# A transformer block's query and key projections: activations or weights standing, and the way to the attention stacks

## The chip, the cores and the metric

The kernel runs on one core of a Trainium2 chip. The metric is the device time of the whole program in microseconds (us). The core has five engines with a queue each: TensorE (PE) multiplies matrices and writes to PSUM, VectorE (DVE), ScalarE (ACT) and GpSimd (POOL) compute on elements, SyncE (SP) issues the transfers (DMA) between DRAM and SBUF, all from one queue here. A queue is served in order, and the engines wait for each other by semaphores.

## The reference

`x` has 8 batches of 1024 tokens, 256 wide. All is float32.

```
x = x + 0.5 * ffn(layernorm(x))
x = x + attention(layernorm(x))
x = x + 0.5 * ffn(layernorm(x))

attention(x):
    kv_c = rmsnorm(x @ W_kv) * g_kv          # 64 wide
    q_c  = x @ W_q                           # 128 wide
    k_content, v = kv_c @ W_kdec, kv_c @ W_vdec     # 16 heads of 16
    q_content    = q_c @ W_qdec                     # 16 heads of 16
    k_rope, q_rope = rope(x @ W_krope), rope(q_c @ W_qrope)   # 16 heads of 32
    q, k = concat(content, rope)             # 48 per head
    softmax(causal(q @ k.T / sqrt(48))) @ v, all heads @ W_o
rope(x) = x * cos + concat(-x2, x1) * sin    # x1, x2: the halves of the 32
ffn(x) = x @ W.T + b + a mixture of 8 rank-16 experts, the best 2 by a gate
```

## The kernel before, in words

The attention is cut into 32 quads `g`: 4 heads of one batch, 1024 tokens. Each quad's queries and keys lie as stacks in SBUF, the 48 dimensions of a head on partitions and tokens along the row, in two tensors `st[g % 2]` that take turns. To keep float32 precision with the fast one-pass matrix form (fp32r), every value is stored as a high part and a low part: a query stack holds both, 48 rows each, `k1_st` the same, and `k2_st` holds the key's parts exchanged, so that two products (L689 and L691) give a score. One further row carries the shift, minus the largest score of each query, and is multiplied by ones.

A quad passes through these steps, named by their letters in the tables that set the order:

- projection (P, "proj", L740 to L746), one per 128 tokens: the latents of the 128 tokens stand as weights, and `wq_s` (192 columns), `wkr_s` (128, in two products) and `wkv_s` (128) stream past. The result, queries, keys and values in one PSUM bank `wp_b`, has tokens on partitions. ACT copies it (L788, L789) to `qk` and `v_s`, and POOL rotates it (L1058 to L1063).
- turn (T, "turn", L758): four transposes per 128 tokens bring dimensions onto partitions, two heads side by side, in the PSUM bank `tp_b`. ACT writes the high parts (H, L801) and DVE the low parts (L, L910), twice each on 48 partitions. Two transfers of 384 KB for each half of the tokens make `k2_st` of `k1_st` (L578, L579).
- maxima (X on PE at L719, M on DVE at L866 and L869): 48 products of queries with keys, and the largest of each row; then the fold (f), a transpose (F, L725), and the shift goes through DRAM to its row (s on SP, L585 and L589).
- scores (S at L689 and L691, E on ACT at L779), 48 pairs, in the two banks of `st_b`, the mask (K on POOL, L1046), values (V, L707), and the reading of the result (o).

Quads overlap: while the scores of one run, the maxima of the next one or two and the projections of a third stand between them. Beside them run the jobs (J): a job is 512 tokens of the first feed-forward net with the latents, or of the output projection with the second net. Its products all use one PSUM bank, `wj_b`. The latents of a job go to DRAM (`nx_scratch`, `kv_scratch`) and come back as `cur` and `kvc` when the batch before has been projected. The first two jobs run in two lanes side by side, as do the last two; the second lane's buffers lie in `probs`.

What sets the order is a table of letters for each engine, `ORDER`, written out for the whole program (`walk` reads it). PE, for example, takes the next score pair for each S. An instruction's waits follow from what it reads and writes.

## Time and profile before

| | |
|---|---|
| median of 3 runs | 2090.83 us (2090.56 to 2091.69) |
| the profiled execution | 2084.36 us, of which its span (first to last instruction) 2082.6 |
| granted TensorE clock, mean | 0.989 of full |
| busy: PE, PE weight loads | 1996.6 us (96%), 1552.6 (75%) |
| busy: DVE, ACT, POOL | 1665.1 (80%), 1258.9 (60%), 973.2 (47%) |
| DMA | 132.32 MB, mean 64 GB/s |

Busy time is the time in which an engine has at least one instruction running. On PE instructions overlap, so a matmul's duration (start to end) is longer than the distance to the next one. The chain of waits, which follows the work that ended last back through the program, gives that distance. In a row of the groups by line the count of a float32 product is twice that in the code: such a product is two instructions, one with fp32r operands or a transpose is one.

### The profile page before, as it was taken

What the parts mean: (1) busy time and instruction counts of PE and PEld (TensorE: products, weight loads), DVE (VectorE), ACT (ScalarE), POOL (GpSimd) and SP (SyncE); (2) the same over time, 40 slices, a digit from 0 to 9 for tenths busy, and PEclk for the clock granted to TensorE, in tenths of its full rate; (3) what the DMA queues carried; (4) which work ended last, traced back from release to release, by engine and by line L of the source; (5) the groups of instructions that cost most, each with busy time, mean ns of one, the idle gap of its engine ahead of it and who ended that gap; (6) DMA issues with size and microseconds to landing.
All of it is one profiled execution on the core that took longest, in us unless ns stands there. A gap on an engine that the chain in (4) does not pass through costs nothing.

```text
span 2082.6 us, 38517 instructions
## 1 busy us (share of the span) xinstructions
PE 1996.6 (96%) x13248; PEld 1552.6 (75%) x13248; DVE 1665.1 (80%) x4924; ACT 1258.9 (60%) x2857; POOL 973.2 (47%) x1574
## 2 busy tenths in 40 slices
PE   4899999999999999999999999999999999999995
PEld 3677777777777777777877787777777777777654
DVE  4698888888888878888788888888788888888842
ACT  4466676665666656666666665666566665566650
POOL 5554554544545545445444445454454554434421
PEclk9999999999999999999999999999999999999996
DMA  2121311222212322123212232213321232221111
GB/s 80 44 62 45 103 35 47 63 89 82 57 32 69 95 67 57 51 56 107 68 42 72 59 94 60 64 47 101 83 58 32 65 93 73 67 68 42 40 28 43
DMA packets 71665, 132.32 MB, mean 64 GB/s; under 512 B 9840, under 2 KB 28528, under 8 KB 71472
## 3 DMA queue, kind: packets, MB, share of 16 engines
q1 hardware_dynamic: 71472, 129.87, 23.2%
q8 instruction: 106, 1.74, 0.4%
q14 instruction: 87, 0.71, 0.1%
HBM read 40.97 MB, written 38.54 MB: 38 GB/s over the span
## 4 chain that ended last, share of the span: by engine, by line
PE 83%; DVE 7%; DMA 3%; ACT 3%; issue 2%; POOL 1%; SPq 0%; POOLq 0%; DVEq 0%; ACTq 0%
PE mx_b L719 13%; PE st_b L689 13%; PE st_b L691 12%; PE o_b L707 11%; PE wj_b L651 5%; PE tp_b L758 5%; PE wp_b L743 5%; PE wp_b L740 4%; PE wj_b L622 3%; PE wj_b L653 3%; PE wj_b L640 3%; PE wp_b L746 2%; DVE st L910 2%; PE wj_b L633 2%; DMA aoc<-ao_scratch 2%
## 5 line engine op out<-in xcount | busy, mean ns | idle before, releaser
L779 ACT ACTIVATE probs<-st_b 128x512 f32<-128x512 f32 (+3 forms) x1536 | 700.5, 490 | 525.4 <-PE st_b L691 497.3
L689 PE MATMUL st_b<-st 113*128 113x512 f32 (+2 forms) x1536 | 558.1, 369 | 7.9 <-ACT probs L779 5.2
L866 DVE CUSTOM_DVE_ANT_0 mx_b<-mx_b,tri 128x256 f32<-128x256 f32 (+3 forms) x1024 | 512.2, 514 | 51.5 <-PE mx_b L719 43.7
L719 PE MATMUL mx_b<-st 112*128 112x256 f32 (+2 forms) x1536 | 532.7, 390 | 4.0 <-DVE mx_s L866 1.8
L691 PE MATMUL st_b<-st,k_st 112*128 112x512 f32 (+2 forms) x1536 | 527.5, 349 | 0.0
L1058 POOL TENSOR_TENSOR rot_c<-qk,cos_s 128x256 f32<-128x256 f32 x256 | 188.9, 738 | 567.8 <-ACT v_s L789 567.7
L869 DVE TENSOR_REDUCE mx_s<-mx_b 128x1 f32<-128x512 f32 (+1 forms) x512 | 334.5, 653 | 88.5 <-PE mx_b L719 82.6
L910 DVE TENSOR_TENSOR st<-tp_b,st 48x512 fp32r<-48x512 f32 x512 | 352.4, 688 | 44.3 <-ACT st L801 30.7
L719 PEld LDWEIGHTS mx_b<-st 112*128 112x128 f32 x1536 | 272.0, 191 | 111.9 <-issue 53.6
L689 PEld LDWEIGHTS st_b<-st 113*128 113x128 f32 x1536 | 291.3, 190 | 62.4 <-ACT probs L779 22.0
L801 ACT ACTIVATE st<-tp_b 48x512 fp32r<-48x512 f32 x512 | 302.6, 591 | 49.0 <-PE tp_b L758 38.4
L1046 POOL TENSOR_SCALAR_AFFINE_SELECT probs<-probs 128x512 f32<-128x512 f32 x256 | 163.9, 640 | 322.1 <-ACT probs L779 321.9
L691 PEld LDWEIGHTS st_b<-st,k_st 112*128 112x128 f32 x1536 | 292.7, 191 | 21.1
L707 PE MATMUL o_b<-probs,v_s 128*17 128x512 f32 (+3 forms) x3072 | 285.0, 489 | 3.4 <-POOL probs L1046 3.0
L1063 POOL TENSOR_TENSOR qk<-rot_c,rot_s 128x256 f32<-128x256 f32 x256 | 189.0, 738 | 20.1
L707 PEld LDWEIGHTS o_b<-probs,v_s 128*17 128x17 f32 x3072 | 70.5, 96 | 141.2 <-issue 111.1
L758 PE MATMUL tp_b<-ident,qk 128*112 128x128 f32 x1024 | 155.2, 273 | 2.3 <-DVE shift L884 1.9
L743 PE MATMUL wp_b<-wkr_s,cur 128*128 128x128 f32 x1024 | 155.9, 275 | 0.0
L788 ACT ACTIVATE qk<-wp_b 128x384 f32<-128x384 f32 x256 | 126.0, 492 | 44.3 <-PE wp_b L746 41.6
L743 PEld LDWEIGHTS wp_b<-wkr_s,cur 128*128 128x128 f32 x1024 | 147.7, 191 | 0.0
L866 DVE DVE_READ_ACCUMULATOR2_ANT mx_s<- 128x1 f32 x1024 | 137.9, 135 | 2.0
L758 PEld LDWEIGHTS tp_b<-ident,qk 128*112 128x112 f32 x1024 | 121.4, 134 | 22.0 <-issue 5.8
(151 smaller groups left out, 2537.9 us busy)
## 6 DMA issues: line engine op xcount, KB each, us to landing
k_st<-st SPq DMA_DIRECT2D x128, 384.0 KB, 6.1
nx_scratch<-stg SPq DMA_DIRECT2D x14, 768.0 KB, 3.5
cur<-nx_scratch SPq DMA_DIRECT2D x14, 768.0 KB, 4.7
ao_scratch<-o_f SPq DMA_DIRECT2D x256, 32.0 KB, 1.7
xa<-in_x SPq DMA_DIRECT2D x15, 512.0 KB, 4.8
x_scratch<-xa SPq DMA_DIRECT2D x15, 512.0 KB, 2.6
xa<-x_scratch SPq DMA_DIRECT2D x15, 512.0 KB, 4.0
aoc<-ao_scratch SPq DMA_DIRECT2D x15, 512.0 KB, 5.8
```

The source lines that it names most:

```text
L689: nc.tensor.matmul(dst, k1_st[u][0:SHIFT + 1, a, P * j:P * j + P], q_st[u][0:SHIFT + 1, a, q0:q0 + w], start=True, stop=False)
L691: nc.tensor.matmul(dst, k2_st[u][0:SHIFT, a, P * j:P * j + P], q_st[u][0:SHIFT, a, q0:q0 + w], start=False, stop=True).then_inc(st_full, 1)
L707: last = nc.tensor.matmul(o_b[32 * a:32 * a + DV + 1, 0, q0 - HALF * h2:q0 - HALF * h2 + n], v_s[q][:, j, a, :], probs[:, a, PLACE[s]:PLAC ...
L719: nc.tensor.matmul(mx_b[:, m % 2, 0:w], q_st[u][0:SHIFT, a, P * i:P * i + P], k1_st[u][0:SHIFT, a, k0:k0 + w], start=True, stop=True).then ...
L743: nc.tensor.matmul(wp[:, HQ:2 * HQ, DC:DQ], cur[:, k, kk * P:(kk + 1) * P], wkr_s[:, kk, q, :].rearrange("p (a c) -> p a c", c=DR), start= ...
L758: last = nc.tensor.transpose(tp_b[0:TURN, 0, P * c:P * c + P], flat[:, P * c:P * c + TURN], ident[:, :])
L779: nc.scalar.activation(probs[:, a, PLACE[s]:PLACE[s] + n], st_b[:, a % 2, HALF - n:HALF], ACT.Exp, scale=SCALE).then_inc(exp_done, 1)
L801: nc.scalar.activation(heads(st[g % 2][rows], e, k), tp_b[rows, 0, :].rearrange("p (s y n) -> p s y n", s=2, n=P), ACT.Copy).then_inc(hi_d ...
L866: nc.vector.tensor_tensor_reduce(src, src, tri[:, HALF - n:HALF], 1.0, NEG, ALU.add, ALU.max, dst).then_inc(mx_done, 1)
L869: nc.vector.tensor_reduce(dst, src, AX_X, ALU.max).then_inc(mx_done, 1)
L910: last = nc.vector.tensor_tensor(heads(st[g % 2][other], e, k), tp_b[rows, 0, :].rearrange("p (s y n) -> p s y n", s=2, n=P), heads(f32(st ...
L1063: nc.gpsimd.tensor_tensor(d[:, :, DC:DQ], rot_cos, rot_sin, ALU.add).then_inc(roped, 1)
```

## The change

- Weights stand. A job's latents stay in SBUF (`stg`, `kvs`), and a unit is 512 tokens, 8 of the 16 heads, and one side, queries or keys: 64 units. Each has three pieces of 128 rows by 512 tokens: the first halves of the 8 heads' rotated dimensions, the second halves, and the content. A query piece is one product with `wq_s` as weights; of a key unit the first two pieces are two products each with `wkr_s`, the third one with `wk_s`. The weights are sorted into this order once, at the start (ACT, "sort").
- Pieces come out with dimensions on partitions, in `tp_b`. So the turns are gone. ACT copies pieces 0 and 1 ("raw"), the rotation is six operations of 128 by 512 on POOL ("rope"; on DVE for two early units), and high and low parts are made on 128 partitions: the content's from PSUM, the rotated in one instruction of 1024 columns each. The cosines and sines are transposed once into `cos_t` and `sin_t`.
- The stacks come from DRAM: a unit's high and its low part are stored (768 KB each) to `q_scratch` or `k_scratch`, and each half of a quad's `st` is loaded by four transfers of 384 KB, its `k2_st` by two. `k2_st` is one tensor now, not two, and the row of ones is written once.
- Values have products of their own ("v", L834), two of 256 columns per 256 tokens.
- Each lane's jobs have two PSUM banks in turn; `wp_b` is gone.
- The tables of all five engines are new, and the jobs of the two kinds alternate.

```diff
-JOBS = [(JOB_A, 0), (JOB_A, 1)]
-for g in range(QUADS + 2):
-    b, q = divmod(g, NQ)
-    if q < 2 and b + 1 < B:
-        JOBS.append((JOB_A, 2 * b + 2 + q))
-    elif q >= 2 and 0 < b < B - 1:
-        JOBS.append((JOB_C, 2 * b + q - 4))
+for b in range(B - 1):
+    for half in range(2):
+        JOBS.append((JOB_A, 2 * b + 2 + half))
+        if b:
+            JOBS.append((JOB_C, 2 * b - 2 + half))
...
+UNIT = [(m, 0, side) for m in range(2) for side in range(2)] + [(m, 1, side) for m in (1, 0) for side in range(2)]
+UNIT += [(m, pair, side) for m in range(2, 2 * B) for pair in range(NP) for side in range(2)]
...
-        "XXSSVXXSSVXXSSPXSXSJXSXSTSXSXJFSSXXJSSXXTSSXXVSSXXPSSXXTSSVSXXSTSXXSPXSXSVXSXSTSXSXPXSXJSXSXJFSXXSJXXSTJ"
+        "XXSSPXXSSJXSSXPXSXSXJSSXJXSXFSXVXXSSJXXSSPXXSSVXXSSPXSXSPXXSSXPXSSXXFJSXSXPXXSSXVXXSSJXXSSJXXSSVXXSSPXXS"
...
+        def rope(engine, n):
+            r, k = rot[SPARE[n]], in_set(n)[0]
+            cols = slice(HALF * (UNIT[n][0] % 2), HALF * (UNIT[n][0] % 2) + HALF)
+            cs, sn = cos_t[:, cols], sin_t[:, cols]
+            engine.tensor_tensor(r[:, 2, :], r[:, 0, :], cs, ALU.mult)
+            engine.tensor_tensor(r[:, 3, :], r[:, 1, :], sn, ALU.mult)
+            engine.tensor_tensor(r[:, 0, :], r[:, 0, :], sn, ALU.mult)
+            engine.tensor_tensor(r[:, 1, :], r[:, 1, :], cs, ALU.mult).then_inc(rot1[SPARE[n]], 1)
+            engine.wait_ge(rot1[SPARE[n]], k + 1)
+            engine.tensor_tensor(r[:, 2, :], r[:, 2, :], r[:, 3, :], ALU.subtract)
+            engine.tensor_tensor(r[:, 1, :], r[:, 1, :], r[:, 0, :], ALU.add).then_inc(roped[SPARE[n]], 1)
...
+                elif name == "qk":
+                    g, half = n, arg[0]
+                    if g > 1:
+                        sp.wait_ge(exp_done, UNITS * (g - 2 + half) + (0 if half else HQ * 2 * HT))
+                    landed(sp, g, half)
+                    b, q = divmod(g, NQ)
+                    cols = slice(HALF * half, HALF * (half + 1))
+                    for side in range(2):
+                        for hl in range(2):
+                            sp.dma_start(f32(st[g % 2])[DQ * hl:DQ * (hl + 1), side, :, cols],
+                                         qk_d[side][b % 2, hl, HQ * DQ * q:HQ * DQ * (q + 1), cols].rearrange(
+                                             "(a r) t -> r a t", a=HQ)).then_inc(qk_in[g % 2][half], 16)
                 elif name == "k2":
                     g, half = n, arg[0]
-                    sp.wait_ge(tp_free, tp_use("turn", g, HT * half + HT - 1) + 1)
-                    k1, k2, cols = f32(st[g % 2])[:, 1], f32(k2_st[g % 2]), slice(HALF * half, HALF * (half + 1))
-                    sp.dma_start(k2[0:DQ, :, cols], k1[ODD:SHIFT, :, cols]).then_inc(k2_in[g % 2][half], 16)
-                    sp.dma_start(k2[ODD:SHIFT, :, cols], k1[0:DQ, :, cols]).then_inc(k2_in[g % 2][half], 16)
+                    if g:
+                        sp.wait_ge(exp_done, UNITS * (g - 1 + half) + (0 if half else HQ * 2 * HT))
+                    landed(sp, g, half)
...
+                    dst = tp_b[:, 0, :].rearrange("p (t c) -> p t c", c=P)
+                    eight = slice(PH * DP * pair, PH * DP * (pair + 1))
+                    if side == 0:
+                        last = nc.tensor.matmul(dst, wq_s[:, k, eight], own.stg[:, :, 2 * P:3 * P], start=True, stop=True)
+                    elif k < 2:
+                        for kk in range(KD):
+                            last = nc.tensor.matmul(dst, wkr_s[:, kk, k, eight], own.stg[:, :, P * kk:P * kk + P],
+                                                    start=(kk == 0), stop=(kk == KD - 1))
+                    else:
+                        last = nc.tensor.matmul(dst, wk_s[:, eight], own.kvs[:, :, :], start=True, stop=True)
...
+                    dve.wait_ge(hir_done, g + 1)
+                    hi, lo = hl_t[SPARE[g]]
+                    nc.vector.tensor_tensor(lo[:, 0:2, :], rot[SPARE[g]][:, 1:3, :], hi[:, 0:2, :].bitcast(F32),
+                                            ALU.subtract).then_inc(lor_done, 1)
```

On PE near the middle of the program the order before has projections (L740 to L746) and turns (L758) between the maxima (`mx_b`) and score pairs (`st_b`):

```order
L758 MATMUL tp_b<-ident,qk 112x128 x4
L740 MATMUL wp_b<-wq_s,cur 128x4x48
L743 MATMUL wp_b<-wkr_s,cur 128x4x32 x2
L746 MATMUL wp_b<-wkv_s,kvc 128x4x2x16
L719 MATMUL mx_b<-st1 128x256
L719 MATMUL mx_b<-st1 128x512
L689 MATMUL st_b<-st0 128x384
L691 MATMUL st_b<-st0,k2_st0 128x384
```

In the changed kernel two pieces of a key unit stand in such places, each in two products of 512 columns:

```order
L755 MATMUL st_b<-st0 128x512
L757 MATMUL st_b<-st0,k2_st 128x512
L824 MATMUL tp_b<-stg,wkr_s 128x512 x2
L787 MATMUL mx_b<-st1 128x512
L787 MATMUL mx_b<-st1 128x384
L755 MATMUL st_b<-st0 128x512
L757 MATMUL st_b<-st0,k2_st 128x512
L755 MATMUL st_b<-st0 128x512
L757 MATMUL st_b<-st0,k2_st 128x512
L787 MATMUL mx_b<-st1 128x512
L824 MATMUL tp_b<-stg,wkr_s 128x512 x2
```

Between two pieces there is at least a score pair or a maximum, and no transpose of projected values is left. On SP, in the middle of the program, the order before has the exchanged copies (`k2_st`), the shift's two steps and the result's stores for one quad and its neighbour:

```order
L578 DMA k2_st0<-st0 48x4x512
L579 DMA k2_st0<-st0 48x4x512
L585 DMA shift_scratch<-shift 16x128
L589 DMA st0<-shift_scratch 1x4x512
L597 DMA ao_scratch<-o_f 16x512 x4
L578 DMA k2_st1<-st1 48x4x512
L579 DMA k2_st1<-st1 48x4x512
L597 DMA ao_scratch<-o_f 16x512 x4
```

In the changed kernel the queue has, around one quad's loads:

```order
L613 DMA q_scratch<-hi_t 384x1x512
L613 DMA q_scratch<-lo_t 384x1x512
L624 DMA st1<-q_scratch 48x4x512 x2
L624 DMA st1<-k_scratch 48x4x512 x2
L635 DMA k2_st<-k_scratch 48x4x512 x2
L613 DMA k_scratch<-hi_t 384x1x512
L613 DMA k_scratch<-lo_t 384x1x512
L643 DMA shift_scratch<-shift 16x128
L624 DMA st1<-q_scratch 48x4x512 x2
L624 DMA st1<-k_scratch 48x4x512 x2
L647 DMA st0<-shift_scratch 1x4x512
L635 DMA k2_st<-k_scratch 48x4x512 x2
```

Stores of units and loads of stacks now stand among the shift's two steps, and the shift's load (L647) waits for its store (L643) in the same queue as they do.

## Rows read from the trace of the kernel before

**Rows 1.** The page's busy time, share of the span, instructions.
```profile
PE 1996.6 (96%) x13248; PEld 1552.6 (75%) x13248; DVE 1665.1 (80%) x4924; ACT 1258.9 (60%) x2857; POOL 973.2 (47%) x1574
```

**Rows 2.** The page's chain that ended last, share of the span by engine, by line.
```profile
PE 83%; DVE 7%; DMA 3%; ACT 3%; issue 2%; POOL 1%; SPq 0%; POOLq 0%; DVEq 0%; ACTq 0%
PE mx_b L719 13%; PE st_b L689 13%; PE st_b L691 12%; PE o_b L707 11%; PE wj_b L651 5%; PE tp_b L758 5%; PE wp_b L743 5%; PE wp_b L740 4%; PE wj_b L622 3%; PE wj_b L653 3%; PE wj_b L640 3%; PE wp_b L746 2%; DVE st L910 2%; PE wj_b L633 2%; DMA aoc<-ao_scratch 2%
```

**Rows 3.** The steady stretch: length, busy per engine, PEclk, DMA share, GB/s.
```profile
290.00:1764.00 1474.00, 1458.66 (x9841) 1144.76 (x9840) 1231.25 (x3641) 925.65 (x2126) 707.19 (x1149) 1.00 0.25 67
```

**Rows 4.** The chain of waits, 1026 to 1049: start, us, what.
```profile
1026.63 0.33 PE wp_b L740 x2
1026.96 0.45 PE wp_b L743 x4
1027.40 0.22 PE wp_b L746 x2
...
1028.89 0.44 PE tp_b L758 x4
...
1041.58 0.23 PE st_b L689
...
1046.17 0.87 PE wj_b L651 x4
```

**Rows 5.** The same chain near 1184.
```profile
1183.98 1.72 PE wj_b L659 x4
```

**Rows 6.** Groups by line and shape, PE: count, busy, mean ns.
```profile
L743 PE MATMUL wp_b<-wkr_s,cur 128*128 128x128 f32 x1024 | 155.9, 275 | 0.0
L758 PE MATMUL tp_b<-ident,qk 128*112 128x128 f32 x1024 | 155.2, 273 | 2.3 <-DVE shift L884 1.9 <-DVE st L910 0.3
...
L740 PE MATMUL wp_b<-wq_s,cur 128*128 128x192 f32 x512 | 128.7, 332 | 4.5 <-ACT v_s L789 4.1
L651 PE MATMUL wj_b<-w_s,xt 128*128 128x256 f32 x480 | 126.8, 387 | 3.0 <-ACT xn L841 1.7 <-DVE xa L1007 1.3
L746 PE MATMUL wp_b<-wkv_s,kvc 128*128 128x128 f32 x512 | 99.5, 276 | 0.0
...
L659 PE MATMUL wj_b<-stg,wkvq_s 128*128 128x512 f32 x56 | 26.3, 592 | 0.0
```

**Rows 7.** Groups by line and shape, ACT and DVE.
```profile
L801 ACT ACTIVATE st<-tp_b 48x512 fp32r<-48x512 f32 x512 | 302.6, 591 | 49.0 <-PE tp_b L758 38.4
...
L910 DVE TENSOR_TENSOR st<-tp_b,st 48x512 fp32r<-48x512 f32 x512 | 352.4, 688 | 44.3 <-ACT st L801 30.7
```

**Rows 8.** Groups by line and shape, POOL.
```profile
L1058 POOL TENSOR_TENSOR rot_c<-qk,cos_s 128x256 f32<-128x256 f32 x256 | 188.9, 738 | 567.8 <-ACT v_s L789 567.7
...
L1086 POOL TENSOR_TENSOR xn<-hl,gate 128x512 f32<-128x512 f32 x30 | 32.8, 1095 | 18.2 <-DVE gate L999 18.1
```

**Rows 9.** DMA queue q1: packets, MB, share of 16 engines' span.
```profile
q1 hardware_dynamic: 71472, 129.87, 23.2%
```

**Rows 10.** Issues by line: count, KB each, median us to landing.
```profile
k_st<-st SPq DMA_DIRECT2D x128, 384.0 KB, 6.1
nx_scratch<-stg SPq DMA_DIRECT2D x14, 768.0 KB, 3.5
cur<-nx_scratch SPq DMA_DIRECT2D x14, 768.0 KB, 4.7
...
shift_scratch<-shift SPq DMA_DIRECT2D x64, 8.0 KB, 1.3
```

**Rows 11.** Stretches inside k_st copies (1062), inside loads from ao_scratch (1004.5).
```profile
1062.00:1066.00 4.00, 4.00 (x30) 2.20 (x29) 3.42 (x13) 1.68 (x4) 3.84 (x8) 1.00 0.80 180
...
1004.50:1007.00 2.50, 2.50 (x23) 1.49 (x15) 0.94 (x3) 0.46 (x2) 2.42 (x5) 1.00 0.95 320
```

**Rows 12.** PE in order of time: the first projection, the first maximum.
```profile
65.02 0.55 PE L740 MATMUL wp_b<-wq_s,cur 128*128 128x192 f32 x2
...
79.23 0.79 PE L719 MATMUL mx_b<-st 112*128 112x256 f32 x2
```

More of the change, by code:

```diff
@@ L31 @@
 WIDE = 256
-ODD = 64
-SHIFT = ODD + DQ
+SHIFT = 2 * DQ
 HLW = ER + E
@@ L40 @@
 RT = 9
-TURN = ODD + DQ
 FOLD = 72
 CONST = 2
+NP = 2
+PH = H // NP
+DP = DC
 TWO = 96
@@ L118, with uses @@
+def uses(*steps):
+    out = []
+    for n, (m, pair, side) in enumerate(UNIT):
+        out += [(name, n, *arg) for name, *arg in steps]
+        if side and not pair and m:
+            out += [("v", k, tt) for k in ((0, 1) if m == 1 else (m,)) for tt in range(2)]
+    return out
 ORDER = {
     "PE": (
-        "JJJjJjjjJJjJjjJJJJjjjJjPJPJPjJTJPTPXXTXXXXPXXJTXXJXXTPXJXXTPXXPXXFXXTXXXPXXSTSXXSSXXSSXPXTXSSXXSSXPXTXSS"
-        "VXXSSTPXXSSJXPXJXTJXXVTXXJXXPFXXPXXTJXXSSXXPSXSXTSXSXSXSXPSXXFSVXXSSXTXSSXXSSXPXSXSTSXSXJSXXSJSXSXJXXSSJ"
@@ L283 @@
         "X": quads(*[("mx", m) for m in range(NM)]),
-        "P": PROJ,
-        "T": quads(*[("turn", k) for k in range(TB)]),
+        "P": TABLES + uses(("piece", 0), ("piece", 1), ("piece", 2)),
         "F": quads(("mx_turn", 0), ("mx_turn", 1)),
@@ L312 @@
         "j": lane_jobs(1, FFN_POOL + [("aggr", 1), ("ss",)], FFN_POOL),
-        "B": [("blank", 1, k) for k in range(BLANKS)],
+        "w": [("widen", 0)],
     },
     "SP": {
+        "u": [("store", n, hl) for n in range(NU) for hl in range(2)],
+        "q": quads(("qk", 0), ("qk", 1)),
         "k": quads(("k2", 0), ("k2", 1)),
@@ L336 @@
 for name, g, *arg in walk("PE"):
-    if name in ("turn", "mx_turn"):
+    if name in ("table", "piece", "v", "mx_turn"):
         TP_USE[name, g, arg[0]] = len(TP_USE)
@@ L482, in f32, with wj_of, last_use, landed @@
             return tensor[tuple(slice(None) for _ in tensor.shape)].bitcast(F32)
-        def heads(tensor, e, k):
-            return tensor.rearrange("p s (y e) t -> p s y e t", e=2)[:, :, :, e, P * k:P * k + P]
         def count(n, k):
             return sum(LANE[i] == LANE[n] and (k == 0 or JOBS[i][0] == JOB_A) for i in range(n))
-        def latents(n):
-            if n > 1:
-                return stg[:, :, :], kvs[:, :, :]
-            return cur[:, HT * n:HT * n + HT, :], kvc[0:KR, HT * n:HT * n + HT, :]
-        def blank(u, k):
-            row, value = (ODD - 32, 0.0) if k < 6 else (P - 32, 1.0)
-            flat = k2_st[u].rearrange("p a t -> p (a t)") if k in (4, 5) else st[u].rearrange("p s a t -> p (s a t)")
-            c = 2 * T * (k - 4 if k >= 4 else k)
-            return row, flat[row:row + 32, c:c + 2 * T], value
+        def wj_of(n, name):
+            return lanes[LANE[n]].banks[bank_use(n, name) % 2]
+        def last_use(m):
+            return max(tp_use("piece", UNIT_OF[m, NP - 1, 1], 2), tp_use("v", m, 1))
+        def rope(engine, n):
[9 more added lines that the diff above has]
+            engine.tensor_tensor(r[:, 1, :], r[:, 1, :], r[:, 0, :], ALU.add).then_inc(roped[SPARE[n]], 1)
+        def landed(sp, g, half):
+            b, q = divmod(g, NQ)
+            units = [UNIT_OF[2 * b + half, q // (NQ // NP), side] for side in range(2)]
+            if g == 1:
+                units += [n for n in range(NU) if SPARE[n]]
+            for part in range(2):
+                for i in range(2):
+                    mine = [in_set(n)[0] for n in units if SPARE[n] == i]
+                    if mine:
+                        sp.wait_ge(hl_out[i][part], 16 * (max(mine) + 1))
         @block.sync
@@ L580, in _ @@
+                    landed(sp, g, half)
+                    b, q = divmod(g, NQ)
+                    cols = slice(HALF * half, HALF * (half + 1))
+                    for hl in range(2):
+                        sp.dma_start(f32(k2_st)[DQ * (1 - hl):DQ * (2 - hl), :, cols],
+                                     qk_d[1][b % 2, hl, HQ * DQ * q:HQ * DQ * (q + 1), cols].rearrange(
+                                         "(a r) t -> r a t", a=HQ)).then_inc(k2_in[half], 16)
                 elif name == "shift":
@@ L1034, in _ @@
                            allow_small_or_imprecise_dtypes=True)
-            for i in range(NQ):
-                last = nc.gpsimd.memset(v_s[i][:, :, :, :], 1.0)
-            last.then_inc(const, 1)
+            nc.gpsimd.memset(v_s[0][:, :, :, :], 1.0).then_inc(const, 1)
             pool.wait_ge(const, CONST)
             for name, g, *arg in walk("POOL"):
-                own = lanes[LANE[g]]
+                own = lanes[LANE[g % NJ]]
                 if name == "mask":
```

615 lines of the change are left out of this document (330 added, 285 removed).

## The prediction

> **What bounds the kernel now.** I read the page's busy times first: PE has work in 96% of the span, DVE in 80%, ACT in 60% [rows 1]. Then the chain that ended last, since a share of busy time says nothing of who waits: it runs on PE for 83% of the span, on DVE for 7%, and the projections and turns have 5 + 5 + 4 + 2 = 16% of it, the low parts (`st`, L910) 2% [rows 2]. Then one long stretch, 290 to 1764 us: PE is busy for 1458.7 of 1474, at full clock, DVE for 84% [rows 3]. So the middle of the program is a queue of matmuls with hardly a gap, and what leaves that queue is what the change is worth. The reader should then see that a matmul's price is not its duration. A turn lasts 273 ns and the groups give the turns 155.2 us busy [rows 6], but on the chain four of them take 0.44 us, 110 ns each [rows 4], for the rest is overlapped by the next one. I price PE by distances on the chain.
>
> **PE, out.** One projection is 0.33 + 0.45 + 0.22 us, one turn 0.44 [rows 4]: 1.44 us, times 256 is 369 us. That is 18% of the span, near the chain's 16%.
>
> **PE, in.** A float32 product of 512 columns is two instructions, and four of these take 1.72 us [rows 5], 0.43 each. 32 query units of three products and 32 key units of five make 256 products, 512 instructions, 220 us. The values are 64 products of 256 columns, 128 instructions at 0.87 / 4 us [rows 4], 28 us. 16 transposes for the tables, 2 us. Together 250 us. The columns that stream past are as many as before (256 x 576 = 256 x 512 + 64 x 256), so nearly all of the difference, 119 us, is the turns. It counts in full only where PE was the chain; by the chain's 16% instead of 18% it is about 105. I take 112, bounds 100 to 119. Two instructions of 512 columns could also be dearer than in rows 5: busy time over count is 26.3 / 56 = 0.47 us [rows 6], which would take 20 us back; I take the chain's price.
>
> **DVE and ACT.** Out go 512 low-part instructions, 352.4 us, and 512 high-part ones, 302.6 [rows 7]. In come, per unit, one PSUM difference of 512 columns (0.69 us by L910) and one of 1024 (at most twice that): 64 x 2.07 = 132 us, so DVE loses some 220 of its 1665 us. ACT gets 128 raw copies, 64 content parts and 32 value copies of about 0.6 us and 64 copies of 1024 columns, at most 1.2: 211 us, against the 302.6 and the copies out of `wp_b`. The reason is the shape: 128 rows where there were 48. These engines hide behind PE for the most part, so this pays only in the 7% of the chain that is DVE's, 146 us, 2% (42 us) of it L910 itself [rows 2]. Bounds 0 and 146; I take 30, nearest to L910's own share, since the rest belongs to the maxima, which stay.
>
> **POOL.** Out go four operations per projection, two of 738 ns and two of about half the size. In come 62 times six of 512 columns: by L1086 1.1 us each, by doubling L1058 1.48 [rows 8], 409 to 550 us in all against some 600. Nothing is gained, as POOL was 47% busy [rows 1]; but one rotation now holds its queue for 7 to 9 us, and masks stand behind it, for which the value products wait. The order places about one rotation per 30 us; I count this in the new waits below.
>
> **The start.** From the first projection to the first maximum passed 14 us [rows 12]. Now the way is: pieces 0.9 us each, two raw copies 0.6, a rotation 7 to 9, a high part 1, a store 3.5, four loads; `cur<-nx_scratch`, 768 KB, landed in 4.7 [rows 10], so 6 or 7 for twice that. That is about 21 us, 7 later, though query pieces can begin before the key latents are done, and PE has more other work to do first. Bounds 0 and 20; I take 8. The table of letters shows the last two lanes' work nearly as before, and the second PSUM bank can save a microsecond or two there; I take nothing.
>
> **The transfers, where I see the risk.** Stacks: 64 halves x 6 loads of 384 KB = 151 MB; stores: 128 x 768 KB = 101 MB. Out go the copies to `k2_st`, 50 MB, and the latents' way through DRAM, 26 MB. From 132 MB it becomes about 308, 9.6 per quad. The queue's 129.87 MB took 23.2% of the span [rows 9], 3.7 us per MB; at that, 308 MB are 1,146 us, 58% of the new span. Before, no matmul of the middle depended on a transfer of this size just in time. Now four loads fill half of `st` after the scores of the quad two earlier have left it and before the first maximum of the new one. I counted PE's work between these two in the new order with the distances of rows 4 (512-column pairs 0.47 us, a job's products 0.2 each): 12 to 20 us in the steady part, with 13 in one quad of four; for `k2_st`, now single, 15 to 27, for the shift 37 to 42 and 17 to 24. How long the four loads take is not in the trace; the nearest rows are transfers of like rows of 2 KB. The copies to `k2_st`, also on 48 partitions, moved 180 GB/s, loads from `ao_scratch` on 128 partitions 320 [rows 11]. 1.57 MB are 8.7 or 4.9 us, with some 1.3 for a small one's way [rows 10]: 6 to 10 us, within 12. With two stores of the same size in front, 11 to 19, which is within the lead at 320 and over it at 180. I take the faster side, since source and destination are different memories here as for `ao_scratch`, and 10 us in all for new waits (these, `tp_b`'s single bank between pieces, the masks); bounds 0 and 170 (below).
>
> The Trainium skill ("DMA: Bandwidth & Descriptors", section "Anatomy of one DMA") fits a transfer by 2.0 us plus its bytes at 436 GB/s. For 768 KB that is 3.8 us, and the store of `nx_scratch` took 3.5 [rows 10]; for the second of the copies to `k2_st` it would be 3.8 as well, counted from the first, where the row has 6.1. By the rule the four loads would take an estimated 5.6 us and never be waited for; by the copies' row they would take 10. It agrees with my forecast, and the copies' row is the rival's.
>
> **Sum.** Against the profiled execution of 2084.4: -112 (PE) - 30 (DVE on the chain) + 8 (start) + 10 (new waits) = 1960. The median of the runs was 6.5 above that execution, so 1967.
>
> **Rivals.**
>
> *The loads come too late.* Slower than before. For: 2.3 times the bytes, one queue, the shift's load waits for its store in SP's queue (1.3 us in rows 10, several times that behind megabytes) and holds up all that follows; at 180 GB/s 308 MB would take 1,710 us. Then half of the 64 halves have stores in front and wait 19 - 13 = 6 us or so at worst, the others less; with queueing I take 5 us for 32 halves: 160 us, on top of which the forecast's 10 goes. 1967 + 150 = 2117. It decides from a rate under about 220 GB/s. Against: leads of 12 us and more everywhere, and the 320 GB/s row. A milder form, a few us in one quad of four and short waits for `tp_b`, gives +20 to +100, 1990 to 2070.
>
> *Busy time is the right price.* By the groups, out go 155.9 + 155.2 + 128.7 + 99.5 = 539 us, in come 512 x 0.47 + 128 x 0.264 = 274 [rows 6]: 265 less, 1820, as a median 1826. Against: 539 us would be 26% of the span where the chain has 16%. A lesser form, in which most of DVE's 146 us on the chain goes with its load, gives 1967 - 100 = 1870 to 1920.
>
> The Trainium skill ("Trainium Kernel Development and Optimization", section "Performance Expectations") says that matmul busy time is a bad metric, because matmuls are pipelined. The trace agrees, 273 ns against 110 for a turn; whoever took busy times all the same would say 1826.
>
> *The change doesn't thin PE's queue.* Not so here: the order shows 5572 rows on PE for 6350, and no transposes but the jobs', the tables' and the shift's.
>
> **Chances.** The forecast, 1925 to 2005: 0.62. Some waits for loads or banks, 2005 to 2087: 0.16. Within 0.2% of before, which is what a measurement of this kernel can tell from no change: 0.02. Late loads, over 2095: 0.12. Under 1925: 0.08. So faster 0.86, same 0.02, slower 0.12. The range, 1915 to 2070, leaves out late loads and the busy-time price; the likeliest case alone is 1925 to 2005.
>
> **What would show it.** In the new trace: four 512-column instructions on the chain in 1.72 us, and no other line's distance changed; PE busy near 96 to 98% with about 110 us less; L910's kind of work at some 130 us and DVE under 76%; no line of waits of PE for a DMA on `st` or `k_st` over some 10 us in total; DMA share near 0.55 to 0.6; the first maximum at about 87 us. Wrong would be: PE idle before L787 or L755 for DMAs for tens of us, landing times of the `st` loads over 12 us, or a PE queue that stands at the pieces for ACT's copies out of `tp_b`.

## The result, and the profile after

| | before | changed |
|---|---|---|
| median (range) | 2090.69 us (2087.92 to 2091.69) | 2005.82 us (2005.07 to 2010.95) |
| ratio, 95% interval | | 0.961, 0.959 to 0.963 |
| profiled execution; its span | 2084.36; 2082.6 | 2005.28; 2002.8 |
| granted clock, mean | 0.989 | 0.980 |

The changed kernel is 85 us faster. The forecast was 1967, so it misses 39 us of what was expected, inside the range of 1915 to 2070. The page of the changed kernel, its busy times and its chain by engine and by line, answers to [rows 1, 2]:

```profile
PE 1901.2 (95%) x10832; PEld 1325.5 (66%) x10832; DVE 1439.5 (72%) x4555; ACT 1024.3 (51%) x2125; POOL 849.4 (42%) x912
...
PE 68%; DMA 10%; DVE 8%; POOL 7%; ACT 2%; issue 2%; SPq 1%; POOLq 0%; DVEq 0%; ACTq 0%
PE st_b L755 12%; PE o_b L775 11%; PE mx_b L787 11%; PE st_b L757 10%; PE tp_b L824 4%; PE wj_b L712 4%; DMA st<-k_scratch 3%; PE tp_b L821 3%; PE wj_b L681 2%; PE wj_b L714 2%; DMA q_scratch<-lo_t 2%; PE wj_b L699 2%; DVE xn L1077 2%; PE wj_b L692 2%; DVE mx_b L977 1%
```

PE lost 95 us of busy time, DVE 226, ACT 235. The chain ran on PE for 83% of the span and now for 68%: DMA and POOL have taken 17% of it where they had 4%. The steady stretch, 290 to 1700, with the columns of [rows 3]:

```profile
290.00:1700.00 1410.00, 1381.70 (x8063) 974.61 (x8056) 1061.65 (x3351) 751.93 (x1578) 636.16 (x673) 1.00 0.65 162
```

PE is busy for 98.0% of it, 99.0% before, and DVE for 75%, 84% before. The chain of waits near 1203 has the price of the new products, as [rows 4, 5]:

```profile
1201.87 0.23 PE st_b L755
1202.10 0.23 PE st_b L757
...
1203.10 0.86 PE tp_b L821 x2
```

The groups by line and shape, to be held against [rows 7, 8]:

```profile
L1030 DVE TENSOR_TENSOR lo_t<-rot,hi_t 128x1024 fp32r<-128x1024 f32 x62 | 78.3, 1264 | 21.7 <-ACT hi_t L907 21.4
...
L1025 DVE TENSOR_TENSOR lo_t<-tp_b,hi_t 128x512 fp32r<-128x512 f32 x62 | 42.4, 684 | 16.2 <-DMA q_scratch<-lo_t 10.7 <-ACT hi_t L901 5.3
...
L907 ACT ACTIVATE hi_t<-rot 128x1024 fp32r<-128x1024 f32 x62 | 65.6, 1058 | 104.3 <-POOL rot L529 104.1
...
L523 POOL TENSOR_TENSOR rot<-rot,cos_t 128x512 f32<-128x512 f32 x62 | 79.1, 1276 | 148.6 <-ACT rot L872 148.5
```

and from the page, over all shapes, the value products:

```profile
L775 PE MATMUL o_b<-probs,v_s 128*17 128x512 f32 (+3 forms) x3072 | 285.7, 490 | 2.0 <-POOL probs L1169 1.9
```

The low parts take some 121 us where they took 352. ACT stands at the high parts for POOL's rotation, 104 us in 52 of them, and DVE at the low parts for ACT. The DMA queue and the issues, as [rows 9, 10]:

```profile
q1 hardware_dynamic: 169648, 305.53, 61.0%
...
st<-q_scratch SPq DMA_DIRECT2D x128, 384.0 KB, 5.9
st<-k_scratch SPq DMA_DIRECT2D x128, 384.0 KB, 8.7
k_st<-k_scratch SPq DMA_DIRECT2D x128, 384.0 KB, 10.4
```

PE's waits for these loads, from the list of waits (us in all, times, longest), are small:

```profile
PEld mx_b L787 <- DMA st<-k_scratch: 4.4, 7, 1.2
...
PE mx_b L787 <- DMA st<-k_scratch: 2.5, 4, 1.0
```

**Where the 85 us are.** The two profiled executions differ by 80 us. I divided each at the first maximum of quad 4 and that of quad 28; the end goes to PE's last instruction. Between the two maxima I added PE's instructions at their usual distance at full clock (0.43 us for 512 columns as one of the two instructions of a float32 product, 0.11 for a transpose, and so on) and call the rest PE's waits; some 15 us of these stand ahead of value products in every kernel.

| us | to quad 4 | 24 quads | PE's work in them | PE's waits in them | the end |
|---|---|---|---|---|---|
| before | 289.8 | 1474.3 | 1401.9 | 72.4 | 313.9 |
| changed | 302.4 | 1400.7 | 1307.1 | 93.7 | 295.2 |

So the work left as priced (95 of an expected 24/32 x 119 = 89 us), but the waits, which I had expected to fall, rose by 21, and the start took 13 us more. (Profiled executions of kernels with the same start differ there by up to 4 us.) Spread evenly over the quads, with the start's 8 us outside them, the forecast's saving of 124 us is an estimated 99 in the 24 quads and 25 outside; measured are 74 (95 less 21) and 6.

**The clock is part of these waits.** The granted clock fell from 2.4 to 1.2 GHz for short stretches, and what PE lost there counts as waiting above. The changed kernel has three of them in the 24 quads, at 903.0, 1107.8 and 1578.8 us; PE, busy for 98% of the steady stretch, had been busy for 5.0 of the 7.0 us ahead of the first and for 5.9 of the 7.8 ahead of each of the others. The first one, as a stretch with the columns of [rows 3], then on the chain:

```profile
903.00:906.40 3.40, 3.40 (x7) 2.04 (x8) 1.97 (x11) 0.60 (x1) 1.25 (x2) 0.50 0.05 16
```

```profile
902.94 0.98 PE mx_b L787 x2
903.91 0.43 PE st_b L755
904.35 0.42 PE st_b L757
904.77 1.71 PE tp_b L821 x2
```

A score product takes 0.43 us there for 0.23, two pieces' instructions 1.71 for 0.86. All such stretches together, from the clock records of each trace (us at the lower level):

| us at 1.2 GHz | to quad 4 | in the 24 quads | the end |
|---|---|---|---|
| before | 10 | 3 | 31 |
| changed | 37 | 10 | 31 |

At most half of a stretch is lost. So the changed kernel lost up to 17 us more to the clock than the kernel before, up to 14 of them before quad 4, where its start is 13 us longer. Where the clock fell after PE had stood, a wait cost twice; how much of the start's 13 us is the one and how much the other, no run separates.

### The profile page after: what moved, and what is told of

The parts are those of the page before. It is cut to its first block, busy times and chain, and to the rows that moved or that the text cites. A ratio compares the mean times of both kernels' runs of the same rounds, so it can differ in the third digit from the quotient of the medians.

```text
span 2002.8 us, 32215 instructions
## 1 busy us (share of the span) xinstructions
PE 1901.2 (95%) x10832; PEld 1325.5 (66%) x10832; DVE 1439.5 (72%) x4555; ACT 1024.3 (51%) x2125; POOL 849.4 (42%) x912
## 4 chain that ended last, share of the span: by engine, by line
PE 68%; DMA 10%; DVE 8%; POOL 7%; ACT 2%; issue 2%; SPq 1%; POOLq 0%; DVEq 0%; ACTq 0%
PE st_b L755 12%; PE o_b L775 11%; PE mx_b L787 11%; PE st_b L757 10%; PE tp_b L824 4%; PE wj_b L712 4%; DMA st<-k_scratch 3%; PE tp_b L821 3%; PE wj_b L681 2%; PE wj_b L714 2%; DMA q_scratch<-lo_t 2%; PE wj_b L699 2%; DVE xn L1077 2%; PE wj_b L692 2%; DVE mx_b L977 1%
## 5 line engine op out<-in xcount | busy, mean ns | idle before, releaser
L755 PE MATMUL st_b<-st 97*128 97x512 f32 (+2 forms) x1536 | 588.2, 387 | 10.6 <-ACT probs L859 6.8
L787 PE MATMUL mx_b<-st 96*128 96x256 f32 (+2 forms) x1536 | 565.5, 411 | 12.4 <-DVE mx_s L980 6.3
L757 PE MATMUL st_b<-st,k_st 96*128 96x512 f32 (+2 forms) x1536 | 533.4, 351 | 0.0
L787 PEld LDWEIGHTS mx_b<-st 96*128 96x128 f32 x1536 | 282.0, 191 | 169.6 <-issue 80.1
L755 PEld LDWEIGHTS st_b<-st 97*128 97x128 f32 x1536 | 293.1, 191 | 134.7 <-issue 61.4
L757 PEld LDWEIGHTS st_b<-st,k_st 96*128 96x128 f32 x1536 | 294.9, 192 | 33.0 <-issue 9.8
L712 PE MATMUL wj_b<-w_s,xt 128*128 128x256 f32 x480 | 123.9, 380 | 1.3 <-ACT xn L951 1.3
L824 PE MATMUL tp_b<-stg,wkr_s 128*128 128x512 f32 x240 | 114.9, 601 | 1.6 <-ACT rot L872 0.9
L1192 POOL TENSOR_TENSOR xa<-xa,hb_s 128x256 f32<-128x256 f32 x120 | 93.1, 802 | 24.8 <-DVE xn L1077 24.8
L1077 DVE TENSOR_SCALAR xn<-xa,mv,rs 128x256 f32<-128x256 f32 x180 | 95.4, 577 | 7.0 <-POOL rs L1185 5.8
## 6 DMA issues: line engine op xcount, KB each, us to landing
k_st<-k_scratch SPq DMA_DIRECT2D x128, 384.0 KB, 10.4
```

What stands on the lines that cost most here:

```text
L712: nc.tensor.matmul(dst, xt[:, tk, P * kk:P * kk + P], w1_s[:, kk, 0:D], start=(kk == 0), stop=False)
L755: nc.tensor.matmul(dst, k1_st[u][0:SHIFT + 1, a, P * j:P * j + P], q_st[u][0:SHIFT + 1, a, q0:q0 + w], start=True, stop=False)
L757: nc.tensor.matmul(dst, k2_st[0:SHIFT, a, P * j:P * j + P], q_st[u][0:SHIFT, a, q0:q0 + w], start=False, stop=True).then_inc(st_full, 1)
L787: nc.tensor.matmul(mx_b[:, m % 2, 0:w], q_st[u][0:SHIFT, a, P * i:P * i + P], k1_st[u][0:SHIFT, a, k0:k0 + w], start=True, stop=True).then ...
L824: last = nc.tensor.matmul(dst, wkr_s[:, kk, k, eight], own.stg[:, :, P * kk:P * kk + P], start=(kk == 0), stop=(kk == KD - 1))
L1077: last = nc.vector.tensor_scalar(own.xn[:, tk, :], own.xa[:, tk, :], own.mv[:, tk, 0:1], own.rs[:, tk:tk + 1], ALU.subtract, ALU.mult)
```

## The experiments

Ratios are to the kernel before, run on the same chip; the changed kernel's is 0.961. More, faster and slower by so many us are against the changed kernel, for few_turns against the kernel before: the difference of the two ratios times 2088 us, good to some 5 us. "Waits" are those of the 24 quads as above, from one profiled execution each, and hold what the clock took: the 24 quads had no stretch at 1.2 GHz in few_turns, add_turns and short_rope, 10 us in light_loads, free_high and shift_first as in the changed kernel, 24 in dve_even, 27 in early_rope, 31 in late_low and one_bank, 48 in late_high and 65 in dve_back. Up to half of each figure is in the waits.

**The turns put back, in the changed kernel.**

```diff
+                    for c in range(5):
+                        nc.tensor.transpose(tp_b[:, 0, P * (c % 4):P * (c % 4) + P], ident[:, :], ident[:, :])
                     dst = tp_b[:, 0, :].rearrange("p (t c) -> p t c", c=P)
```

> The changed kernel with five transposes of 128 columns (of the identity, into tp_b, overwritten by the piece that follows) ahead of each of its 192 pieces: PE gets back about the instructions that the turns were, 960 of 0.11 us by the distances on the chain, 106 us, and no other engine gets any work. Theory A (PE's queue is what the kernel is made of, also after the change, and work in it counts in full): 90 to 110 us more than the changed kernel. Theory B (the removed instructions had partly filled time in which PE would have waited for DVE or ACT, so the waits grew when they went, some 20 to 30 us): the same instructions put back hide those waits again, 60 to 85 us more. Theory C (transfers set the pace of the changed kernel): under 50 us more.

2062.6 us, ratio 0.988 (0.986 to 0.990), 56 us more. That is between theory C and the 60 to 85 of theory B. Half of the 106 us came back as time. In the 24 quads PE's work grew by 78 us and its waits fell by 34, from 94 to 60.

**Turns taken out, in the kernel before.**

```diff
-                    for c in range(HALF // P):
+                    for c in range(HALF // P if g < 2 else 1):
                         last = nc.tensor.transpose(tp_b[0:TURN, 0, P * c:P * c + P], flat[:, P * c:P * c + TURN], ident[:, :])
```

> The kernel before, in which from the third quad on one of the four transposes of a turn is made (the result is not the reference's); 720 transposes of 0.11 us by the distances on the chain are gone, 79 us, and nothing else. Theory A (instructions leaving PE's queue count in full): 72 to 80 us faster than before. Theory B, after add_turns, where 106 us came out as 57: a part of the turns filled time in which PE would wait for DVE and ACT, whose load is larger here than in the changed kernel: 25 to 50 us faster.

2057.1 us, ratio 0.984 (0.982 to 0.986): 33 of 79 us. In the 24 quads the work shrank by 63 us, the waits grew by 38. Both runs say the same, and the lists of waits show where. PE's weight loads for the maxima, waiting for DVE to empty a bank, in the kernel before:

```profile
PEld mx_b L719 <- DVE mx_s L869: 17.8, 36, 0.9
...
PEld mx_b L719 <- DVE mx_s L866: 11.8, 34, 0.9
```

in the kernel before with fewer turns:

```profile
PEld mx_b L719 <- DVE mx_s L869: 28.7, 65, 0.9
PEld mx_b L719 <- DVE mx_s L866: 26.0, 85, 0.9
```

in the changed kernel:

```profile
PEld mx_b L787 <- DVE mx_s L977: 30.9, 98, 2.3
PEld mx_b L787 <- DVE mx_s L980: 26.9, 65, 2.5
```

and in the changed kernel with the turns put back:

```profile
PEld mx_b L787 <- DVE mx_s L979: 17.6, 54, 1.2
PEld mx_b L787 <- DVE mx_s L982: 11.4, 32, 1.5
```

30, 55, 58, 29 us: the sum follows the turns, whichever kernel they stand in. For the score pairs, waiting for ACT, it is 22, 40, 46 and 28. So it is theory B's mechanism in both runs: the turns were filler for PE's waits as much as work.

**DVE's load put back, in lumps and evenly.** Six maxima of 512 columns per unit, two behind the content's low part and four behind the rotated one's:

```diff
+                    if extra[0]:
+                        dve.wait_ge(ex_done, extra[0])
+                    for e in range(4):
+                        nc.vector.tensor_reduce(ex_s[:, e:e + 1], cos_t[:, HALF * (e % 2):HALF * (e % 2) + HALF],
+                                                AX_X, ALU.max).then_inc(ex_done, 1)
+                        extra[0] += 1
...
```

> The changed kernel with six additional maxima of 512 columns per unit on DVE (read from cos_t, result unused), two behind the content's low part and four behind the rotated one's: some 0.6 us each, 3.6 per unit, 220 us more busy on DVE, which is what the change took from it. PE, ACT, POOL and the transfers get nothing. Theory A (of the prediction, the load taken from DVE paid about 30 us): 25 to 50 us more. Theory B (DVE's load was hidden by PE's queue and taking it paid nothing): under 10 us more. Theory C (DVE's load is what the maxima wait for, so that a us of it shows nearly in full): 100 us or more.

2160.9 us, ratio 1.035 (1.033 to 1.038), 155 us more, slower than the kernel before. Waits 216, of which 110 ahead of maxima (20 in the changed kernel). Next, the same work singly (`if m % 4 == 3:` behind a maximum, one `tensor_reduce`):

> As dve_back the changed kernel with some 220 us of additional maxima on DVE (384 of 512 columns, 0.6 us each, from cos_t, unused), but single, one behind every fourth maximum, where dve_back had lumps of 1.2 and 2.4 us behind the low parts and came out 155 us slower. Theory A (DVE's queue is long in all, so what it is given shows wherever it stands): 100 us slower or more. Theory B (a lump longer than two banks of maxima can cover was the cost): 20 to 60 us slower.

2038.4 us, ratio 0.976 (0.974 to 0.978), 31 us more; waits 121, 35 ahead of maxima. DVE was busy for 1656 us in the one and 1620 in the other. So it is theory B of the second run: the lump was the cost, by a factor of five. While DVE is away for 1.2 or 2.4 us, PE fills the two banks of `mx_b` and stands. Up to 27 us of the 122 by which the waits of dve_back exceed the changed kernel's are the clock (65 us at 1.2 GHz for 10), the most of all runs.

**Loads lightened.**

```diff
+                            part = slice(HALF * half, HALF * half + 16) if hl and g > 1 else cols
-                            sp.dma_start(f32(st[g % 2])[DQ * hl:DQ * (hl + 1), side, :, cols],
+                            sp.dma_start(f32(st[g % 2])[DQ * hl:DQ * (hl + 1), side, :, part],
...
```

> The changed kernel in which, from the third quad on, the loads of the low parts (of st and of k2_st) move 16 of 512 columns: of 151 MB of loads about 70 are not moved, and the low parts in the stacks are stale, so the result is not the reference's. The number of transfers and of waits stays. Theory A (after the start the loads are never late): within 6 us of the changed kernel. Theory B (the loads, or the bytes in the way of the shift and of the stores, hold back the scores or take time from the other engines): 20 us or more faster.

1987.8 us, ratio 0.952 (0.951 to 0.954), 18 us faster: between the two theories, nearer to B. Waits 81, so 12 of the 18 us are in the steady part. No engine worked faster (DVE 1436.0 us busy, ACT 1025.0, POOL 849.6), so the bytes cost only by coming late, and not at PE alone: DVE's wait for the store of a low part (`lo_t <- DMA q_scratch<-lo_t`), 10.7 us in the changed kernel, is gone, and that for a job's input (`bst <- DMA xa<-in_x`) is 7.1 for 10.4. And the chain by engine of this kernel reads:

```profile
PE 78%; POOL 8%; DVE 8%; ACT 2%; DMA 2%; issue 2%; SPq 0%; POOLq 0%; DVEq 0%
```

DMA's share went from 10% to 2%, 160 us of chain for 18 us of time: a second chain lay close behind it.

**Rotations shortened.**

```diff
-            engine.tensor_tensor(r[:, 3, :], r[:, 1, :], sn, ALU.mult)
-            engine.tensor_tensor(r[:, 0, :], r[:, 0, :], sn, ALU.mult)
...
-            engine.tensor_tensor(r[:, 2, :], r[:, 2, :], r[:, 3, :], ALU.subtract)
```

> The changed kernel with three of the six operations of each rotation left out (the result is not the reference's): POOL holds its queue for some 3.7 us per unit where it was 7.5, about 230 us of its load go. Theory A (POOL's rotations are off the chain, except at the start, where one stands between the first piece and the first maximum): 4 to 10 us faster, all of it before 300 us. Theory B (masks behind the rotations, and ACT, whose queue stands at the high part while POOL rotates, 104 us in sum, hold back the scores): 20 to 50 us faster, spread over the whole span.

1966.2 us, ratio 0.942 (0.940 to 0.945), 39 us faster. Quad 4 begins 11 us sooner, and waits are 66: 27 us of the gain are in the steady part. Theory B in size, but it doesn't tell the masks from ACT's queue, nor either from the unit's way to DRAM. Three runs were to do that.

**High and low parts that don't wait for the rotation.**

```diff
+                        act.wait_ge(roped[SPARE[g]], in_set(g)[0])
...
-                    act.wait_ge(roped[SPARE[g]], done + 1)
+                    if g < 12:
+                        act.wait_ge(roped[SPARE[g]], done + 1)
...
-                    nc.scalar.activation(hl_t[SPARE[g]][0][:, 0:2, :], rot[SPARE[g]][:, 1:3, :], ACT.Copy).then_inc(hir_done, 1)
+                    src = rot[SPARE[g]][:, 1:3, :] if g < 12 else cos_t[:, :].rearrange("p (a t) -> p a t", t=HALF)
+                    nc.scalar.activation(hl_t[SPARE[g]][0][:, 0:2, :], src, ACT.Copy).then_inc(hir_done, 1)
...
```

> The three left-out operations of short_rope gave 40 us, 27 of them in the steady part. Here POOL keeps all six, but from unit 12 on ACT's high part of the rotated pieces (hi_r) and DVE's low part (lo_r) read cos_t, which nobody writes, instead of the rotation's result, so neither waits for POOL (the result is not the reference's); the next unit's first copy waits for the rotation instead. Theory A (ACT's queue stands at hi_r until POOL has rotated, the exponentials behind it come late, and the scores wait for st_b): 15 to 30 us faster than the changed kernel, and PE's waits ahead of score pairs fall. Theory B (the masks and the router's work behind a rotation in POOL's queue come late): within 6 us of the changed kernel, since POOL's queue is the same.

1998.1 us, ratio 0.956 (0.954 to 0.959), 10 us faster, with an interval of about 4 to 16: neither theory's number. Waits ahead of score pairs fell from 21 to 14 us, as A has it, and those of the steady part as a whole from 94 to 88. ACT's standing is a part, not the whole, of short_rope's 39.

**ACT's high parts up to three exponentials later.** The table of letters for ACT, here one of its rows (H is the high part of the rotated pieces, E an exponential):

```diff
-        "EEJEECEECEECEEEEHEEJCEEEECEEJEECEEJEEJHEEEEJEECEEJEECEECEECEEJEECEEHEEEEEEEECEEEECEEJJEECEEHJEEJEEEECEEJ"
+        "EEJEECEECEECEEEEEEHJCEEEECEEJEECEEJEEJEEEHEJEECEEJEECEECEECEEJEECEEEEEHEEEEECEEEECEEJJEECEEHJEEJEEEECEEJ"
```

> Only ACT's table is changed: 39 of the 64 high parts of rotated pieces stand up to three exponentials later (never past a copy or a job's step, so 25 stay); all is computed. Theory A (ACT stands at them for POOL): these 39 no longer wait, 8 to 20 us faster than the changed kernel. Theory B (masks or the router's work on POOL are what is late): within 5 us. Theory C (the units' way to DRAM has no slack, so that a later high part makes a later store and a later load): 5 us or more slower.

2077.5 us, ratio 0.994 (0.992 to 0.996), 69 us slower: four fifths of the gain of the change are gone, though only 39 letters moved, each by two or three places. Waits 153, 52 ahead of maxima. Its list of waits has DVE's standing at the low parts, 21.4 us in the changed kernel:

```profile
DVE lo_t L1030 <- ACT hi_t L907: 82.4, 39, 5.4
```

So it is theory C in sign, and its mechanism is at least in part a lump again: DVE stands at the low part and the maxima behind it wait. Up to 19 us of it in the 24 quads are the clock (48 us at 1.2 GHz for 10).

**DVE's low parts up to two maxima later.** One row of DVE's table (L a low part, every second one a rotated one; M a maximum, o a step of reading the result); 44 of the 64 moved:

```diff
-        "MMnMLMMooMMoJoMMJJJJMMJJMMJJMMJMMfMMnMMMMLMoMMooLoJMMJMMJJJMMJJMMMMMMMMMLMMMMLMMJMMfJJMMnJMMJoMMoJMMoJMM"
+        "MMnMMMLooMMoJoMMJJJJMMJJMMJJMMJMMfMMnMMMMLMoMMoooLJMMJMMJJJMMJJMMMMMMMMMLMMMMMMLJMMfJJMMnJMMJoMMoJMMoJMM"
```

> The changed kernel with DVE's table changed: 44 of the 64 low parts of rotated pieces (lo_r) stand up to two maxima (or a step of reading the result) later. late_high, where ACT made the high parts up to three exponentials later, came out 72 us slower, and DVE then stood for 82 us at lo_r where it had stood for 21. Theory A (a step that stands in DVE's queue before its high part is there holds back the maxima behind it): the 21 us go, 3 to 12 us faster than the changed kernel. Theory B (what counted in late_high was the unit's way to DRAM getting longer): 3 to 15 us slower, as the stores and the next unit's copies come later still.

2022.2 us, ratio 0.968 (0.966 to 0.970), 14 us slower. Theory A fails, and the size is theory B's: letting DVE do maxima first only moved the cost. Waits ahead of a half's first maximum, which needs the loads, went from 3 to 8 us, and those of the shift's transpose from 7 to 11. The way from unit to stack seems to have no slack either; but up to 10 of the 14 us are the clock (31 us at 1.2 GHz for 10), so this is argued and not shown.

**The start: the first shift ahead of the second quad's loads.** SP's table; s is a step of the shift, q and k are loads:

```diff
-        "JjJJjuuuuquuuukqqsqsuukJuuJ
+        "JjJJjuuuuquuuuksqsqquukJuuJ
...
```

> The changed kernel with SP's table alone changed at one place at the start: the first quad's first shift (its store and its load) stands ahead of the second quad's eight loads, not behind them. Theory A (at the start the shift's two transfers of 8 KB, 9.4 and 7.2 us in the changed kernel, lie behind megabytes, and the first scores wait for them): the first score comes 8 to 12 us sooner, and the whole is 3 to 10 us faster, the less the second quad's loads then come late. Theory B (the start is paced by what comes before, latents, pieces and rotations): within 3 us.

2011.8 us, ratio 0.964 (0.963 to 0.966), 7 us slower, which neither theory has. The changed kernel's chain of waits between the first maxima and the first score has this:

```profile
104.03 0.29 DVE shift L995
104.34 9.38 DMA shift_scratch<-shift
113.74 7.22 DMA st<-shift_scratch
121.00 0.80 PE st_b L755
```

and the chain of this run, where the shift goes first:

```profile
103.77 0.29 DVE shift L995
104.08 0.32 SPq L643
...
105.89 8.95 DMA st<-k_scratch
...
114.89 0.70 PE mx_b L787
```

PE's order has maxima of the second quad ahead of the first scores. Their loads now started late, and the first score began at 129.6 for 121.0. The 16.6 us of two small transfers had been in plain view on the chain, and weren't to be had by moving them alone.

**One bank for the stages again.**

```diff
-            return lanes[LANE[n]].banks[bank_use(n, name) % 2]
+            return lanes[LANE[n]].banks[bank_use(n, name) % 2 if n < 4 or LANE[n] else 0]
...
-                if name == "wo0" and use:
+                if (name == "wo0" or n >= 4 and not LANE[n]) and use:
```

> The changed kernel, in which the first lane's jobs from the fifth on use one PSUM bank again, as before the change, in the same order of work. Theory A (of the prediction, which gave the second bank nothing): within 5 us of the changed kernel. Theory B (the jobs' products stand in the order so that a bank must be free sooner than it can be read): 15 us slower or more, with PE waiting at wj_b.

2029.1 us, ratio 0.974 (0.972 to 0.975), 26 us slower. Theory B: waits 115, the 21 more standing ahead of the jobs' products (10 before `low1`, 5 before `tr1`, where the changed kernel had next to none). Up to 10 of the 21 are the clock (31 us at 1.2 GHz for 10).

**The rotation begun with the first piece.** The one version that was meant to be better:

```diff
+            engine.wait_ge(tp_free, tp_use("piece", n, 0) + 1)
             engine.tensor_tensor(r[:, 2, :], r[:, 0, :], cs, ALU.mult)
+            engine.tensor_tensor(r[:, 0, :], r[:, 0, :], sn, ALU.mult)
+            engine.wait_ge(tp_free, tp_use("piece", n, 1) + 1)
             engine.tensor_tensor(r[:, 3, :], r[:, 1, :], sn, ALU.mult)
-            engine.tensor_tensor(r[:, 0, :], r[:, 0, :], sn, ALU.mult)
...
```

> The changed kernel, all computed, in which the two operations of a rotation that read piece 0 alone come first and wait for piece 0's copy only; the other four wait for piece 1's, as all six did. POOL has the same work. It stood at rotations for piece 1's copy for 148.5 us in 47 of them, 3.1 us each, and two operations are 2.5 us. Theory A (the length of a unit's way from its pieces to the stacks is what the waits grow from: 3.7 us off each rotation gave 40 us, late_high's lengthening cost 72): 2 us off most rotations, 12 to 28 us faster than the changed kernel, masks no later than before. Theory B (short_rope gained by taking load from POOL, so that masks and the router's steps came sooner): within 5 us.

2015.3 us, ratio 0.965 (0.963 to 0.968), 9 us slower, neither theory's number. The expected effect is there: DVE's wait for the high parts fell from 21.4 to 7.3 us, the waits ahead of score pairs from 21 to 18. But those ahead of the jobs' first transposes rose from 12 to 24 and those ahead of maxima from 20 to 28, with another reason in the trace. The normalisation `xn`, in the groups of the changed kernel and then of this one:

```profile
L1077 DVE TENSOR_SCALAR xn<-xa,mv,rs 128x256 f32<-128x256 f32 x180 | 95.4, 577 | 7.0 <-POOL rs L1185 5.8
```

```profile
L1078 DVE TENSOR_SCALAR xn<-xa,mv,rs 128x256 f32<-128x256 f32 x180 | 129.4, 766 | 7.3 <-POOL rs L1185 6.0
```

Its timeline, first DVE and then POOL, shows why (start, us):

```profile
347.82 0.68 DVE L982 TENSOR_REDUCE mx_s<-mx_b 128x1 f32<-128x512 f32 x1
348.42 2.79 DVE L1078 TENSOR_SCALAR xn<-xa,mv,rs 128x256 f32<-128x256 f32 x2
```

```profile
347.24 1.31 POOL L525 TENSOR_TENSOR rot<-rot,sin_t 128x512 f32<-128x512 f32 x1
348.51 1.28 POOL L527 TENSOR_TENSOR rot<-rot,sin_t 128x512 f32<-128x512 f32 x1
349.75 1.31 POOL L528 TENSOR_TENSOR rot<-rot,cos_t 128x512 f32<-128x512 f32 x1
```

Two instructions of 0.41 us take 2.79 while POOL rotates. By earlier starting, the rotations fell onto more of them, and `xn` took 34 us more of DVE. How much of the 9 us that makes, beside up to 9 us of clock in the 24 quads (27 us at 1.2 GHz for 10), isn't settled.

## Why the prediction was right in direction and 39 us short

- **PE's price: right.** 0.86 us for a piece of two instructions, PE's work in the steady part down by 95 where 89 was priced, the score pairs at 0.23 a product as before.
- **What fails is how much of it counts.** "It counts in full only where PE was the chain", I wrote, and took 112 of 119. Taken out of the kernel before, turns gave 33 of 79 us (42%); put back into the changed one they cost 56 of 106 (53%). At about half, the term is near 55, not 112. The chain's 16% for the projections and turns was no bound from below: a chain names one path, and just behind it lay DVE's and ACT's.
- **DVE and ACT, -30: the size holds for DVE, the form decides.** 220 us of load, spread, cost 31 to put back. ACT's 235 us were put back in no run, so its share of the term isn't shown. But the same load in lumps of 1.2 and 2.4 us costs 155, and the change itself lengthens the low part of the rotated pieces from 0.69 to 1.26 us. I priced busy time, where it is the longest stretch away from the maxima that PE feels.
- **The second bank, "I take nothing": wrong.** It is worth 26 us in this order of work, and I had looked for its effect only at the end.
- **New waits, +10: too small.** The half of a rotation is worth 39 us (11 of them before quad 4), the low parts' loads 18. I had counted the rotation's 7.7 us against the masks. PE waits little for the masks, 2 us ahead of the value products and 6 ahead of their weight loads; it is ACT that stands, for 104 us at the high parts, which free_high makes out to be about 10 of the 39. How the other 29 divide over the way to the stacks and DVE's slowed instructions isn't settled.
- **The start, +8: the first maximum was right, the next step was missed.** The first maximum came at 85.2 us (79.2 before, 87 forecast). The first score came at 121.0 for 105.5, as the shift's two transfers of 8 KB stood 16.6 us behind megabytes. I had named that for the steady part ("several times that behind megabytes") and not counted it here. Nor did any term have the clock: all prices were taken at full clock, and the changed kernel spent 37 us at 1.2 GHz before quad 4, for 10.
- **The rival of late loads** had its mechanism right and its price wrong: landing at 8.7 and 10.4 us is within the leads, and PE waited 7 us for them; the 18 us of light_loads is what lateness cost in all. By the Trainium skill's fit ("DMA: Bandwidth & Descriptors", section "Anatomy of one DMA") the four loads were to take an estimated 5.6 us; that section is on transfers issued by GpSimd, and these come from SyncE. The second pair landed 8.7 us after its issue in the median, nearer to the 10 of the copies' row, and the measurement decides.
- **The marks**, with what I had expected in parentheses. PE 95% with 95 us less (96 to 98% with 110), low parts at 125 us with the few at the start (130), DVE 72% (under 76), waits on stack loads 7 us (under 10), DMA share 0.61 (0.55 to 0.6).

The terms as measured, PE near -55, DVE -31, bank -26 and, the other way, the start 13, loads 18, and 39 for half of the rotations' operations, don't add up to a sum: each was taken alone, and each fills or uncovers the waits of the others. The 85 us are what they make together, and that the total fell inside the range is in part luck: the gain on PE was taken at twice its size and the new waits far too small, and a second bank worth 26 us, taken at nothing, made up for some of it.

## What to carry to other kernels

Where PE was busy 96% of the time and a few per cent of waits stood at short hand-overs to DVE and ACT, turns taken out of PE's queue counted 42% and put back 53%, since they were also filler for these. In a kernel of this kind take the chain's price as the upper end and try half of it by an experiment of this sort before you forecast. Ask of an engine beside the bottleneck how long it is away in one piece, against the banks that cover it, before asking how busy it is. And where five queues are written out in one fixed order, a wait in the trace is no proof that its removal pays: four re-orderings were made here (late_high, late_low, shift_first, early_rope), each aimed at such a wait, and all were slower, by 7 to 69 us. Look at the granted clock of each stretch before you put a difference down to waits alone.

## What the runs showed of the hardware

- Some of DVE's instructions that go from SBUF to SBUF are stretched by POOL's. In the changed kernel, of the 180 `xn`, 131 ran with POOL idle in 0.41 us and 46 with POOL busy beside them for most of their time in 1.08; in early_rope 88 did, in 1.14 us. `o_t<-o_t,o_rc` went from 0.42 to 0.85. Maxima, which read PSUM, took 0.64 and 0.66; but the transposes `o_f<-o_t`, from SBUF to SBUF, also kept their 0.71 and 0.70. The Trainium skill ("SBUF — State Buffer", section "Who interferes with whom") has DVE and GpSimd share one pair of ports by an exclusive lock. The trace agrees in so far as the longest `xn` of the changed kernel took 1.46 us, its own 0.41 and 1.05 more, which is less than one operation of a rotation (1.28); the lock itself no run here shows.
- With 69 MB fewer moved (light_loads), DVE, ACT and POOL were busy for the same time within 0.3%. The same section of the Trainium skill says that DMA doesn't contend with an engine, and this run agrees.
- Between two executions of one kernel, time and granted clock went together: late_low took 2010.9 us at a mean of 0.981 and 2024.0 at 0.975, the changed kernel 2005.1 at 0.982 and 2011.0 at 0.976.
